# Cross attention in 32 batches on one core: new queue orders on all engines around the product G x

## What is computed

```
x_q = (w_qk y)^T            x_k = w_qk x            x_v = w_v x + b_v
attention = softmax(x_q x_k, last axis)             # 1024 x 1024
attention = attention / (1e-07 + attention.sum(axis=1))
x_r = relu(w_t (x - x_v attention) + b_t)
out = x + x_r
```

## Time and profile before

| | us |
|---|---|
| median of 3 runs (2074.06 to 2080.71) | 2077.18 |
| the profiled execution's own time | 2079.49 |
| its span, first to last instruction | 2077.7 |

### The profile page before, as it was taken

One profiled execution on the slowest core, in us unless ns is written; L12 is line 12 of the kernel. 1 busy time (PEld: TensorE's weight loads), 2 busy tenths in 40 slices (PEclk: granted clock), 3 DMA queues, 4 the chain that ended last, 5 costly groups with the idle time before them and its releaser, 6 DMA issues.

```text
span 2077.7 us, 27090 instructions
## 1 busy us (share of the span) xinstructions
PE 1912.0 (92%) x8808; PEld 1574.1 (76%) x8808; DVE 1682.2 (81%) x2096; ACT 1409.7 (68%) x1990; POOL 1074.4 (52%) x583
## 2 busy tenths in 40 slices
PE   5999999999999998999999999999999999999999
PEld 4778777787777787777877778777778777777777
DVE  3878878788878888888788878888887888888877
ACT  3777666776667776676766777666777667776665
POOL 5445555455544545554555545564454554455541
PEclk7999999999999999999999999999999999999999
DMA  4034422344222443223442234432244413344211
GB/s 132 26 102 122 122 61 85 97 121 121 75 87 81 121 121 109 62 81 111 121 121 62 93 88 121 121 95 70 78 121 121 120 52 104 88 121 121 82 40 61
DMA packets 78240, 199.50 MB, mean 96 GB/s; under 512 B 8688, under 2 KB 9712, under 8 KB 78192
## 3 DMA queue, kind: packets, MB, share of 16 engines
q1 hardware_dynamic: 60544, 166.10, 22.6%
q0 software_dynamic: 17360, 32.51, 9.7%
q10 hardware_dynamic: 288, 0.39, 0.1%
HBM read 149.16 MB, written 33.55 MB: 88 GB/s over the span
## 4 chain that ended last, share of the span: by engine, by line
PE 45%; issue 19%; ACT 19%; POOL 11%; DVE 3%; DMA 2%; ACTq 0%; SPq 0%; DVEq 0%; POOLq 0%
PE pv L974 16%; POOL xt_lo L256 8%; PE row_b L836 6%; PE row_a L836 4%; PE row_b L932 4%; PE row_a L932 4%; ACT p_sb L445 4%; PE row_b L888 4%; ACT p_hi L453 4%; PE row_a L888 3%; ACT x_hi L357 3%; PE pv L946 3%; ACT ev L436 2%; DVE res L729 2%; ACT x_sb L371 2%
## 5 line engine op out<-in xcount | busy, mean ns | idle before, releaser
L288 POOL TENSOR_TENSOR y_lo<-y_raw,y_hi 128x896 fp32r<-128x896 f32 (+1 forms) x128 | 283.0, 2233 | 394.9 <-DVE p_lo L678 270.9
L671 DVE SCALAR_TENSOR_TENSOR colsum<-p_sb,row_inv,colsum 128x1024 f32<-128x1024 f32 x224 | 402.4, 1797 | 8.3 <-DVE row_inv L659 0.4
L678 DVE SCALAR_TENSOR_TENSOR p_lo<-p_sb,row_inv,p_hi 128x1024 fp32r<-128x1024 f32 x254 | 326.8, 1302 | 78.3 <-ACT p_hi L453 77.7
L234 POOL TENSOR_TENSOR x_lo<-x_raw,x_hi 128x1024 fp32r<-128x1024 f32 x62 | 151.4, 2441 | 435.7 <-ACT x_hi L357 435.7
L445 ACT ACTIVATE p_sb<-p_sb,neg_max 128x1024 f32<-128x1024 f32 x256 | 293.3, 1149 | 55.0 <-DVE neg_max L651 55.0
L436 ACT ACTIVATE ev<-row_b 128x512 f32<-128x512 f32 x384 | 228.4, 595 | 139.6 <-PE row_b L836 139.0
L453 ACT ACTIVATE p_hi<-p_sb,row_inv 128x1024 fp32r<-128x1024 f32 x256 | 293.0, 1145 | 43.8 <-PE pv L974 43.8
L974 PE MATMUL pv<-p_hi,z_lo 128*128 128x512 f32 x1024 | 295.5, 413 | 0.0
L974 PE MATMUL pv<-p_hi,z_hi 128*128 128x512 f32 x1024 | 281.7, 392 | 14.6 <-DVE res L729 14.4
L974 PE MATMUL pv<-p_lo,z_hi 128*128 128x512 f32 (+1 forms) x1047 | 273.4, 384 | 0.0
L651 DVE CUSTOM_DVE_ANT_0 p_sb<-row_a,ev 128x1024 f32<-128x1024 f32 x128 | 156.5, 1223 | 135.5 <-PE row_a L836 135.1
(11 more groups left out here) (192 smaller groups left out, 4126.4 us busy)
## 6 DMA issues: line engine op xcount, KB each, us to landing
x_sb<-x SPq DMA_DIRECT2D x64, 512.0 KB, 5.9
xt_raw<-x SPq DMA_DIRECT2D x124, 256.0 KB, 5.2
x_raw<-x SPq DMA_DIRECT2D x62, 512.0 KB, 7.1
out<-res SPq DMA_DIRECT2D x62, 512.0 KB, 3.4
y_raw<-y SPq DMA_DIRECT2D x64, 256.0 KB, 4.0
y_raw<-y SPq DMA_DIRECT2D x32, 512.0 KB, 3.8
xt_raw<-x POOLq DMA_DIRECT2D x31, 512.0 KB, 5.4
xt_raw<-xt_raw POOLq DMA_DIRECT2D x62, 256.0 KB, 6.2
```

The source lines that it names most:

```text
L234: nc.gpsimd.tensor_tensor(x_lo[par][:, kt, :], raw, x_hi[par][:, kt, :].bitcast(FP32), ALU.subtract).then_inc(x_lo_done, 1)
L288: nc.gpsimd.tensor_tensor(y_lo[:, of:, cols], y_raw[:, 1 + of:8, cols], y_hi[:, of:, cols].bitcast(FP32), ALU.subtract).then_inc(y_lo_done, 1)
L671: nc.vector.scalar_tensor_tensor(out=colsum[:, :], in0=p_sb[r][:, :], scalar=inv, in1=colsum[:, :], op0=ALU.mult, op1=ALU.add).then_inc(ac ...
L678: nc.vector.scalar_tensor_tensor(out=p_lo[r][:, :], in0=p_sb[r][:, :], scalar=row_inv[:, j:j + 1], in1=p_hi[r][:, :].bitcast(FP32), op0=AL ...
```

## The change

It moves calls in the queues of all five engines, and it splits or narrows three waits. No operation is added or taken out, and no shape is changed.

- SP: the four loads of x's blocks for `xt_raw` are issued ahead of the loads of y, as soon as the last product of G x has read the old ones.
- POOL: `y_sums` ahead of `xt_one`; the low parts in the order xt 0, x 0, xt 1, x 1 instead of x 0, x 1, xt 0, xt 1; `y_low` 1 and 2 wait only for the low part of p of the row (3,0) instead of both, `y_low` 3 for both. In batch 0 the sums of G's blocks (`g_operands`) come ahead of `y_sums`, and their low parts later.
- ACT: `xt_high` 0 ahead of `x_high` 0 in slot t = 2; `xt_high` 1 from slot 3 to the end of slot 2 (the third); `x_bias` of the second half from slot 2 to slot 3; `y_high` 2 and `gx_high_one` go in among the `gx_pass` calls ahead of the last `p_high`, `y_high` 3 stays behind it. In batch 0 `g_operands_high` moves from slot 0 to slot 1.
- DVE: the two additions and `gx_parts` go ahead of the last `p_low`, which sits inside `gx_parts` behind T_2N.
- PE: `gx_p1` waits for the first low half of x only and `gx_p2` for the second; `z_half` 0 no longer waits for all low parts of G x but for the first, and for T_1.

```diff
             def batch(b, par, first=False, last=False):
                 if not last:
+                    if not first:
+                        sp.wait_ge(gx21_full, b)
+                    load_xt(b + 1)
                     sp.wait_ge(y_hi_done, NP * (b + 1))
                     sp.wait_ge(y_lo_done, NP * (b + 1))
                     load_y(b + 1)
-                    if not first:
-                        sp.wait_ge(gx21_full, b)
-                    load_xt(b + 1)
...
+            def g_operands_low():
+                sums = g_sums
                 pool.wait_ge(gs_hi_done, 1)
...
-                    xt_one(b + 1)
+                    if b == 0:
+                        xt_one(b + 1)
+                        g_operands()
                     y_sums(b + 1)
+                    if b > 0:
+                        xt_one(b + 1)
                     xt_two(b + 1)
+                    if b > 0:
+                        y_low(b + 1, 0)
+                    xt_four(b + 1)
                     if b == 0:
-                        g_operands()
-                    y_low(b + 1, 0)
-                    xt_four(b + 1)
-                    for kt in range(KT):
-                        x_low(b + 1, 1 - par, kt)
+                        g_operands_low()
+                        y_low(b + 1, 0)
                     for h in range(2):
                         xt_low(b + 1, h)
+                        x_low(b + 1, 1 - par, h)
+                    pool.wait_ge(p_lo_done, NT * b + NT - 1)
+                    y_low(b + 1, 1)
+                    y_low(b + 1, 2)
                     pool.wait_ge(p_lo_done, NT * (b + 1))
-                    for t in range(1, NP):
-                        y_low(b + 1, t)
+                    y_low(b + 1, 3)
...
                 if t >= 2 and not last:
+                    if t == 2:
+                        xt_high(b + 1, 0)
                     x_high(b + 1, 1 - par, t - 2, early=first)
-                    xt_high(b + 1, t - 2)
                 copy_b(b, t, 2, EV_U3, 1.0)
...
-                if t == 0 and first:
+                if t == 1 and first:
...
-                if 0 < t < 3 and not first and (t == 2 or not last):
-                    x_bias(b, t - 1)
+                if t == 1 and not first and not last:
+                    x_bias(b, 0)
+                if t == (2 if last else 3) and not first:
+                    x_bias(b, 1)
...
                 if t == 2 and not last and not first:
                     y_high(b + 1, 1)
+                if t == 2 and not last:
+                    xt_high(b + 1, 1)
...
                 if t == NP - 1 and not last:
                     gx_pass(b + 1, gx11, gx22, gx22_part, 3 * b + 1, -1.0)
+                    y_high(b + 1, 2)
                     gx_pass(b + 1, ev[:, 3, :], gx12, gx12_part, b + 1, 1.0)
                     gx_pass(b + 1, ev[:, 2, :], gx22, gx22_part, 3 * b + 2, 1.0)
+                    gx_high_one(b + 1)
                 if t == NP - 1:
                     p_high(b, t, 1, first)
...
                 if not last:
-                    gx_high_one(b + 1)
                     gx_pass(b + 1, gx21, gx22, gx22_part, 3 * b + 3, -1.0)
-                    y_high(b + 1, 2)
                     y_high(b + 1, 3)
...
-            def gx_add(b):
+            def gx_add_one(b):
                 dve.wait_ge(gx12_full, b)
                 dve.wait_ge(gx_passed, 4 * b - 1)
                 nc.vector.tensor_tensor(gx12, gx12, ev[:, 2, :], ALU.add).then_inc(gx_added, 1)
+
+            def gx_add_two(b):
                 dve.wait_ge(gx_passed, 4 * b)
                 nc.vector.tensor_tensor(gx22, gx22, ev[:, 3, :], ALU.add).then_inc(gx_added, 1)
...
                 if first:
                     split_hnT()
                 else:
+                    before_low()
                     b_low(b, 1, B_N22, row_a[:, left], -1)
...
+
+            def spread(b):
                 dve.wait_ge(s_shared, (P // Q - 1) * (b + 1))
...
                     turn(b)
-                if b < B - 1 or t < NP - 1:
+                    gx_add_one(b + 1)
+                    gx_add_two(b + 1)
+                    gx_parts(b + 1, before_low=lambda: p_low(b, t, 1))
+                elif b < B - 1 or t < NP - 1:
                     p_low(b, t, 1)
...
                     return
-                gx_add(b + 1)
-                gx_parts(b + 1)
                 col_inverse(b)
+                spread(b)
                 scale(b, 0)
...
             def gx_p1(b, par):
-                pe.wait_ge(x_lo_done, KT * (b + 1))
+                pe.wait_ge(x_lo_done, KT * b + 1)
                 pe.wait_ge(max_done, NT * b)
...
+            def gx_p2(b, par):
+                pe.wait_ge(x_lo_done, KT * (b + 1))
                 raw_product(par, gx11, G_12, 1, 0, False).then_inc(gx11_full, 1)
...
+                    pe.wait_ge(gx_lo_done, 3 * (b + 1) + 1)
+                    pe.wait_ge(t_made, 3 * (b + 1) + 1)
+                    z_half(1 - par, 0)
                     pe.wait_ge(gx_lo_done, 3 * (b + 2))
-                    z_half(1 - par, 0)
```

6 lines of the change are left out of this document (3 added, 3 removed).

## The result

The changed kernel takes **1955.78 us** (median, 1953.65 to 1956.39) where the kernel before took 2078.94 in the same comparison: a ratio of 0.939, 95% interval 0.937 to 0.942. The prediction was 1974 us (range 1885 to 2020), 18 us above what came.

A forecast was written before the change was run, and what follows sets the result against it. PE, busy for 92% of the span, was taken to set the end, so only its waits could be won. 84 us from 31 batches plus 19.5 from the start made 103.5, giving 1974 us, range 1885 to 2020.

The forecast's parts named there:

- The price of a meeting: DVE operation with two SBUF inputs waits for POOL's earlier operation to end, costing up to 2.4 us; POOL's next then waits.
- energy_out of (3,0): DVE operation ahead of gx_p1, made late by meetings with POOL: starts at about 1105.6 instead of 1101.51 in the middle batch.
- PE's wait ahead of gx_p1: New wait of PE for all maxima: gx_p1 starts at 1108.0 instead of 1105.38, a wait of 2.6 us.
- DVE's chain: DVE's operations from energy_out of (3,0) to the next batch's p1: sum 21.2 us, p1 at 1126.84, DVE last by 0.3.
- The first column sum: DVE's L668, 1.69 us in the median, becomes free (0.75), as y_sums no longer waits for xt_one; results come 0.9 earlier.
- the transpose and L696: DVE operations now beside POOL's y_low 1 and 2: taken at no cost, with 1.8 us a batch kept for the range.
- Hidden work: T_3 on POOL starts 2.1 us after the last p_low instead of 6.3; its way to z_high ends under DVE's chain.
- The order of the last p_low: DVE's moved operations, last p_low among them, keep their 8.85 us; that p_low ends at 1119.9, hidden from PE.
- The clock: PE's clock loss from idling, 2.0 us in the mean batch: 1.0 taken, of which 0.65 hides behind DVE's chain and slack.
- The start: Batch 0: waits of 21.1 us (ACT) and 21.9 (PE) go, a new wait of about 2 comes; net 19.5 us.
- one meeting fewer: Rival (0.15): p_low (2,1) gets in ahead of x_low 1, energy_out starts at 1103.4, 58.6 us a batch: 1893 us.
- No meeting: Rival (0.10): energy_out stays at 1101.5, only ACT's x_bias ahead of the last exponentials counts, 57.7 us a batch: 1865 us.

The follow-up runs named there:

- the moved ACT instruction: Changed kernel with ACT's x_bias of the second half back in the third slot (slot 2), ahead of the exponentials: 1884.68 us, ratio 0.905.
- the run with the coarse wait: Changed kernel with POOL's y_low 1 and 2 again waiting for both low parts of p of the last slot: 2143.53 us, ratio 1.031.
- one break: Changed kernel where in batch 0 POOL waits for the end of gs_lo before it takes up y_lo: 1951.67 us, ratio 0.937.
- the added wait: Changed kernel where POOL starts xt_low 1 only when DVE has finished p_low of row (2,1): 1877.42 us, ratio 0.903.

## Why the prediction was right, step by step

**The price of a meeting** was right, and it carries the whole result. A DVE operation with two SBUF inputs ends 1.08 or 1.09 us after the POOL operation that it met, in the rows above. Over the whole span `p_lo` has a mean of 1794 ns, 0.51 above the free 1.28: x 254 that is 4.2 us a batch for two meetings. The rule of the Trainium skill, page "SBUF — State Buffer", section "Who interferes with whom" (the first to ask has the port for the whole instruction) is borne out most sharply by the moved ACT instruction: 0.3 us one way or the other. It is not borne out in batch 0 of the changed kernel: there the column sum's row begins at 47.70, before those of `y_lo` (48.58) and of the three instructions behind it, and all four go ahead of it.

**energy_out of (3,0)** was to start 39.8 us after `p1` and starts 38.95 after it. This is the term that was mis-sized, and the step that failed is the one on the results: "results come 0.9 us earlier, the wait for them (0.20 here) goes". I credited PE with 0.20 and left ACT and POOL at their old times. The same earlier results let SP load the next `x_sb` sooner. ACT's bias in the second slot, first in the kernel before, then in the changed one:

```profile
1083.52 1.16 ACT L371 ACTIVATE x_sb<-x_sb,bias 128x1024 f32<-128x1024 f32 x1 [1.15 <-DMA x_sb<-x]
```
```profile
1069.01 1.15 ACT L381 ACTIVATE x_sb<-x_sb,bias 128x1024 f32<-128x1024 f32 x1
```

It waited 1.15 us for the transfer and now waits for nothing, and the exponentials behind it come earlier: `xt_lo` 0 starts 25.04 us after `p1`, where I had put 25.75. All three meetings follow it. The step is 0.84 us shorter than forecast (60.39 against 61.23): this place has 0.69 of it (0.89 less the 0.20 that I had credited), the clock 0.10, and DVE's chain 0.05 (21.24 in the sum, 21.19 here). That the load is earlier because of the results is read from the two traces and was not tried by itself.

**PE's wait ahead of gx_p1**: 2.6 foreseen, 2.13 there. **DVE's chain** from `energy_out` to `p1`: 21.2 foreseen, 1091.90 to 1113.09 is 21.19.

**The first column sum** L668 was to become free of POOL, and **the transpose and L696** were to cost nothing beside `y_low`. All cases of the first, and the means of the other two (in the changed kernel they are L686, L711 and L714):

```profile
L711 DVE STREAM_TRANSPOSE p_sb<-colsum 128x1024 f32<-128x1024 f32 x31 | 38.6, 1246 | 3.3
L714 DVE TENSOR_REDUCE s_part<-p_sb 128x32 f32<-128x1024 f32 x31 | 37.8, 1220 | 1.1
L686 DVE TENSOR_SCALAR colsum<-p_sb,row_inv 128x1024 f32<-128x1024 f32 x32 | 24.1, 754 | 1.1
```

754 ns where the median was 1688, and 1246 and 1220 with POOL at work beside them. The bound of 1.8 us a batch for them falls.

**Hidden work.** "Its way to `z_high` ends at about 1124.4, under DVE's chain" was a slack of about 1.1 us; the trace has 0.1:

```profile
1110.69 1.01 ACT L441 ACTIVATE z_hi<-row_b 128x1024 fp32r<-128x1024 f32 x1
```

It ends at 1111.70 and `z_lo` starts at 1111.82. It cost nothing here, but the run with the coarse wait shows how near it was: T_3's way and DVE's chain are a tie, and without the finer wait the whole change would be a loss of 3%.

**The order of the last p_low** I had at no effect on the chain; it is worth 19 us. The prediction's sum came out right all the same, since it summed the new order as it is; that this order was part of the gain, it did not see.

**The clock**: I took half of the loss, 0.35 us on the batch; the mean step is 0.25 over the middle batch.

**The start**: 19.5 foreseen, 19.7 where it is made alone, 10.9 in the changed kernel. ACT's waits are as foreseen: 2.38 us instead of 21.11 for the sums of G, and a new one of 2.19 for the transfer into `xt_raw`. Two steps failed. The first is the second half of the price: "and POOL's next waits for it in turn". That was read from one pair of POOL instructions, and it does not hold for a run that starts on a DMA issue; it has 4.9 of the 8.8 us between 59.5 and 68.3, since one break brings `gx_p1` to 63.4. The second is that the sum of the start has no meetings at all. With the break DVE still loses 7.4 us in them (2.41, 3.23 and 6.76 us instead of 1.28, 1.28 and 2.48), with POOL's old order 2.5 (3.78 us for the column sum, the rest free); the other 3.9 us are read from these rows and were not tried by themselves.

So the miss is two terms of opposite sign, and that it is as small as 18 us is in part luck: 28 us more from the batches (106.2 and 6.0 against 84), and 8.6 less from the start. That is 19.6 on the span (1954.6 against 1974.2); the median lay only 0.6 under the profiled execution here, where I had taken 2.3 off. Of the 6.0 behind the last `gx_p1`, 3.6 are the wait for `xt_lo`, and PE is busy for 2.2 us less there with the same work. The rival "one meeting fewer" (1893 us) has the size of what the moved bias brought about (1885), though the meeting that went there is that of `p_low` (2,0) with `xt_low` 1, not the one that the rival named. "No meeting" (1865) comes near what the added wait did (1877), though that took only the two of `p_low` away and left the column sum's. The margins were as thin as the prediction said: 0.31 us between `xt_low` 1 and `p_low` (2,0), where it had 0.3.

## What to carry to other kernels

Where DVE and POOL both read two tensors from SBUF, write down who asks first at each meeting: if DVE is the engine on the path, let POOL wait for a semaphore of DVE's, even if that makes POOL later. After an edit that takes a long wait away, look for the next tie on every chain that ends at the same instruction; here two chains ended within 0.1 us, and one small edit to a wait turned the gain of 6% into a loss of 3%, another into a gain of 10%. A term that is right by itself (the start) can be lost to a neighbour that arrives with it.

## What the runs showed that I had not expected

POOL instructions that follow a DMA issue without a wait begin 0.3 us before the end of the one ahead, and DVE stays shut out for the whole run: 11.31 us in the changed kernel, 9.05 with four instructions behind the issue instead of five. A single wait of POOL for its own last instruction ends that: POOL's operations then take 3.4 us, DVE's column sum 2.4.

Idle time of PE costs clock on top of itself: with 3.6 us of idle PE a batch it is 0.967, with 2.1 it is 0.984, and with nearly none 0.999. In the run with the coarse wait, PE's matmuls took 0.63 us instead of 0.39 behind 4.05 us of idle time, that is 1.2 instead of 2.4 GHz, and this added 1.6 us to a wait of 4.0. A wait of 2.13 us, in the middle batch of the changed kernel, left the mean clock of that batch at 1.00, while over all batches the first matmul of `gx_p1` took between 0.39 and 0.79 us.
